# Ring places freed by a table of last steps for the first 48 chunks of the edge sums

## The reference

```
msg = feat[src] * a[:, :, None]                       # a row of 256 per edge
out = jax.ops.segment_sum(msg, dst, num_segments=N)   # first and last layer of this kind
agg = jax.ops.segment_sum(wbar[:, None] * msg, dst, num_segments=n)   # second: msg from feat[src] + edge features
```

## Time and profile before

| | |
|---|---|
| runs | 6173.45, 6169.5, 6158.29 us; median 6169.5 |
| profiled execution | 6167.76 us, of which the span of the profile is 6166.0 |
| busy in the span | PE 71%, DVE 45%, ACT 15%, POOL 28% |
| gathers in the first sum stage | start 598.9 to 947.8 us |
| gathers in the second sum stage | start 1864.0 to 2219.6 us |
| gathers in the third sum stage | start 5457.7 to 5796.5 us |

### The profile page before, as it was taken

The page is one execution under the profiler, slowest core; times in us unless marked ns, Lnnn a source line. Parts: engine busy times, 40 slices in busy tenths (PEclk is TensorE's granted clock), DMA queues, the critical chain, the costliest instruction groups (busy, mean ns, idle before and its releaser), DMA issues. The chain is left out here.

```text
span 6166.0 us, 74287 instructions
## 1 busy us (share of the span) xinstructions
PE 4377.0 (71%) x17651; PEld 3012.9 (49%) x17653; DVE 2769.8 (45%) x6598; ACT 908.0 (15%) x1973; POOL 1738.7 (28%) x1518
## 2 busy tenths in 40 slices
PE   0695985457916676766898999989936727766539
PEld 0463553235603444633566766667625715434337
DVE  4766445225685555687102011020141256664558
ACT  0200001111000012227102021020212310000012
POOL 2472771126707730100000000000021056547400
PEclk9897996557958787888999999999958968888759
DMA  3383873225818720013542433324222126624300
GB/s 115 104 242 120 266 243 107 72 75 155 244 41 260 240 86 16 3 59 161 178 129 68 139 100 110 122 66 134 64 83 65 57 61 184 195 79 128 94 27 21
DMA packets 438326, 726.18 MB, mean 118 GB/s; under 512 B 58253, under 2 KB 298698, under 8 KB 433698
## 3 DMA queue, kind: packets, MB, share of 16 engines
q1 hardware_dynamic: 318919, 513.08, 26.8%
q0 software_dynamic: 81376, 175.99, 9.5%
q10 hardware_dynamic: 37874, 35.28, 1.7%
HBM read 602.76 MB, written 121.12 MB: 117 GB/s over the span
## 5 line engine op out<-in xcount | busy, mean ns | idle before, releaser
L738 PE MATMUL gin_up_sums<-gin_ring,gin_acc 125*128 125x250 f32 (+1 forms) x4000 | 1069.5, 427 | 23.8 <-ACTq L771 23.8
L738 PEld LDWEIGHTS gin_up_sums<-gin_ring,gin_acc 125*128 125x128 f32 x4000 | 755.7, 189 | 332.0 <-ACTq L771 24.8
L720 DVE BATCH_NORM_STATS2 gin_up_stat<-gin_mlp_z x160 | 77.8, 486 | 1160.4 <-ACT gin_mlp_z L768 1160.2
L2255 POOL IOTA two_seats_pid<- 125x1 f32 x1 | 0.1, 138 | 1617.3 <-ACTq L2252 1617.3
L2824 PE MATMUL edge_sum_part<-edge_ring_rows,edge_sum_hot 128*125 x832 | 275.8, 486 | 142.9 <-DVE edge_sum_hot L1655 118.1
L2824 PE MATMUL loops_sum_part<-loops_ring_rows,loops_sum_hot 128*125 x832 | 272.5, 481 | 122.0 <-issue 81.8
L2940 POOL DMA_INDIRECT edge_ring_rows<-edge_table,src_e x243 | 282.9, 1164 | 239.6 <-PE edge_sum_part L2824 168.6
L2940 POOL DMA_INDIRECT gat_ring_rows<-gat_table,src_e x243 | 276.8, 1139 | 173.4 <-PE gat_sum_part L2824 105.5
L2940 POOL DMA_INDIRECT loops_ring_rows<-loops_table,src_e x243 | 266.3, 1096 | 176.2 <-PE loops_sum_part L2824 109.5
L2824 PEld LDWEIGHTS edge_sum_part<-edge_ring_rows,edge_sum_hot 128*125 128x125 f32 x832 | 164.4, 227 | 254.1 <-issue 234.8
L3170 PE MATMUL adj_counts_part<-adj_counts_far,adj_counts_low 128*128 128x325 bf16 x1032 | 210.4, 338 | 101.6 <-DVE adj_counts_far L3151 51.0
(11 more groups left out here) (800 smaller groups left out, 8008.6 us busy)
## 6 DMA issues: line engine op xcount, KB each, us to landing
gin_ring<-gin_adj SPq DMA_DIRECT2D x100, 937.5 KB, 4.8
gin_ring<-gin_adj SPq DMA_DIRECT2D x100, 625.0 KB, 3.9
edge_sum_own<-edge_attr_in SPq DMA_DIRECT2D x97, 512.0 KB, 4.8
gat_sum_ef<-edge_attr_t_in SPq DMA_DIRECT2D x96, 512.0 KB, 4.4
gin_adj<-adj_counts_tile SPq DMA_DIRECT2D x25, 1562.5 KB, 5.2
gat_logits_places<-lookup SPq DMA_DIRECT2D x32, 800.0 KB
edge_logits_places<-lookup SPq DMA_DIRECT2D x32, 800.0 KB
loops_logits_places<-lookup SPq DMA_DIRECT2D x32, 800.0 KB
```

Of the source, the lines that this page charges most:

```text
L720: v.bn_stats(statf[:, bass.ds(i * 12 + (h * 6 + f * UNITS * 6), 6)], z1f[:, nodes(i, h, f * N)]).then_inc(stats, 1)
L738: mm = pe.matmul(sums[h][k][:, 0:n * P].rearrange("p (t n) -> p t n", n=P), acc[:, t, k * 128:(k + 1) * 128], ring[0:P, q, 0:n, c * P:(c + ...
```

## The change

`prepare` keeps a table `g.free_at` of 48 entries: for old chunk c the first step of chunk c + 1, which is the count of steps after which chunk c is done, plus HOTS. A new function `place_free` reads the entry into a register for old chunks below KNOWN = 48 and waits on `summed` for it; then it increments a semaphore of its own and waits for that. From old chunk 48 on the wait is as before. POOL and SP both call it. The work per chunk, the ring and the order of the gathers stay the same.

```diff
+KNOWN = 48
...
                 v.wait_ge(past_ready, 1)
+                q.mark(v.tensor_scalar(g.free_at[:], begin[0:1, 1:KNOWN + 1], float(HOTS), None, ALU.add))
...
+        place_known, load_known = st.sem("place_known"), st.sem("load_known")
...
-                ahead.gather_rest(pool, ring, summed)
+                ahead.gather_rest(pool, ring, summed, place_known)
...
-                    ahead.load(sp, ring, c, summed, loaded)
+                    ahead.load(sp, ring, c, summed, loaded, load_known)
...
-    def load(self, eng, ring, c, summed, loaded):
+    def load(self, eng, ring, c, summed, loaded, known):
 
         if c in self.FIRST:
-            eng.wait_ge(summed, c + QUAD - 1 - RING + T + HOTS)
+            self.place_free(eng, c + QUAD - 1, summed, known)
...
-    def gather_rest(self, pool, ring, summed):
+    def place_free(self, eng, c, summed, known):
+
+        old = c - RING
+        if old < KNOWN:
+            eng.wait_ge(summed, eng.value_load(self.g.free_at[0:1, old:old + 1], min_val=1 + HOTS, max_val=old + 1 + T + HOTS))
+            eng.sem_inc(known, 1)
+            eng.wait_ge(known, old // QUAD // EVERY + 1 if c - QUAD + 1 in self.FIRST else old // QUAD - old // QUAD // EVERY)
+        else:
+            eng.wait_ge(summed, old + T + HOTS)
+
+    def gather_rest(self, pool, ring, summed, known):
 
         for q in range(RING, CS, QUAD):
             if q not in self.FIRST:
-                pool.wait_ge(summed, min(q + QUAD - 1, CS - 1) - RING + T + HOTS)
+                self.place_free(pool, min(q + QUAD - 1, CS - 1), summed, known)
...
+        g.free_at = sb("free_at", [1, KNOWN], I32)
```

More of the change, by code:

```diff
@@ L1647, in _ @@
                     sp.dma_start(own[:, c % OWN:c % OWN + n, :], feats_v[:, c:c + n, :]).then_inc(own_in[c % OWN // QUAD], 16)
-                    ahead.load(sp, ring, c + 2 * QUAD, summed, loaded)
+                    ahead.load(sp, ring, c + 2 * QUAD, summed, loaded, load_known)
             @block.vector
```

## The result

| | before | after |
|---|---|---|
| median of the runs | 6169.5 us (5 runs, 6158.29 to 6178.77) | 6132.87 us (5 runs, 6126.55 to 6135.61) |
| span of the profile | 6166.0 us | 6131.1 us |

The kernel became 36.6 us faster, a ratio of 0.9942 [0.9932, 0.9953]. Forecast (6137) and result agree to 4 us, but two terms behind it, the reads of the table and the pace of the gathers, were wrong in opposite directions. The stages show them.

The account below looks back on a forecast made before the run. POOL's gathers were taken to bound the three sum stages. 42.6 us won at the 37th gathers less 10.4 given back made 32.2, so 6137 us; own range 6120 to 6149, with rivals 6117 to 6162.

Parts of the forecast that it names:

- What bounds the stages: Three edge-sum stages: POOL never rests from first gather to last, so a stage ends with its last gather plus unchanged tail.
- When the places come free: First gather of each sum stage needs 8 steps instead of 32, so starts 21.0, 17.8 and 17.9 us earlier.
- The gate at chunk 116: The 37th gather still needs 80 steps; from there at most 14.7, 17.8 and 17.0 us can be won.
- The reads: Nine POOL table reads a stage at 0.43 us each, 3.9 us; range from 0 (hidden) to 12.3 us a stage.
- The gain at the 37th gather: How much earlier the 37th gather comes in the three stages: 14.7, 13.9 and 14.0 us, together 42.6.
- What is given back: Behind the 37th gather POOL's slow phase lasts longer, with dearer gathers: 5.3, 1.9 and 3.2 us lost, together 10.4.
- rival 1: First stage: two gathers lock to each TensorE quad, leaving 4.8 us won; with reads at 1.36 us, 6155 us; chance 0.22.
- my own mark for wrong: Signs against the forecast, among them gather distances over 1.65 us in the slow phase of a sum stage.
- The sum: Whole kernel: 42.6-10.4 = 32.2 us won, 6135.6 against the profiled execution, 6137 as median of the runs.
- Nothing comes of it: Rival 2: another server (the tail, DMA at 0.98) holds the stage ends, 6169 us; chance 0.05.
- slower: Rival 3: register waits stall POOL's queue before known quads; slower by 0.3% from 2.40 us each, 6204 at 3; chance 0.04.
- rival 4: Sum stages: reads hidden and little given back, 49.5 us won, 6120 us; chance 0.04.

Follow-up runs that it names:

- with constants: The changed kernel with the same earlier waits written as constants, without table read, increment or second wait: 6130.06 us, ratio 0.9935 to before.
- the experiment with one input: VectorE's multiplication by the weights made a one-input multiplication by 1, in the changed kernel and in the kernel before: 6096.48 and 6121.08 us.
- the cut kernels on the third chip: VectorE's multiplication and addition cut by two or four in the changed kernel, by four in before, by four with 80 known: 6344.09, 6348.87, 6341.7, 6344.9 us.

## Why the prediction was right

- **What bounds the stages: right.** POOL is the server from its first gather to its last. A third fewer gathers shortened the stages by 16%, and from before to after the last gather and the last matmul of a stage moved together to within 0.2 us.
- **When the places come free: right in the steps, short in the release.** The first gathers came at 8.9, 6.3 and 6.5 us into the stages; the forecast has 8.3, 6.0 and 5.8. The release was taken over at 0.28 us; over the register it is 0.85 in every stage, and with constants it is 0.27 again. The 0.57 us were left out of the sum by taking the increment and the second wait at nothing; no run separates them from the wait on a register. Relative to the stages 20.3, 17.5 and 17.2 us are won at the first gather.
- **The gate at chunk 116: right.** POOL waited at it in the first stage alone, and tables of 24 and 80 entries moved it as expected.
- **The reads: the size was off.** Nine reads were to cost 3.9 us a stage and cost none, the bound from below. The row at hand gave the duration rightly (435 ns), but not the place: the reads run beside the gathers. Eight times as many still gave the time of after. With reads at nothing the prediction's own sum is 6169.5-(14.7+17.8+17.0-10.4) = 6130.4, not the 6132 that it names for that case.
- **The gain at the 37th gather: 14.7, 13.9 and 14.0 forecast, 14.6, 15.7 and 15.3 measured.** The reads would have made it more, but the slow phase was slower than taken: 1.572 and 1.539 us a gather instead of 1.522 and 1.488, so 1.8 us over 36 gathers in the second and third stage. 17.5-1.8 = 15.7 and 17.2-1.8 = 15.4 are what was measured, to 0.1. I had carried the pace of before over unchanged.
- **What is given back: 5.3, 1.9 and 3.2 forecast, 8.4, -1.1 and 3.3 measured.** The mechanism is right in the first and third stage: the slow phase lasts longer. VectorE first waits for gathered rows 55 and 38 us behind the 37th gather; the forecast has 54 and 36. In the first stage the price of a slow gather was too small: the 24 gathers behind the 37th came 1.68 us apart instead of 1.574. Ahead of it the lock of rival 1 held for 26 gathers, and my own mark for wrong, over 1.65 us in the slow phase, was passed there with 1.733, or 1.68 without the gate's wait. That pace cost nothing at the 37th gather, because POOL still reached the gate with 2.13 us to wait; the loss is 3 us more than forecast behind it. In the second stage the last 206 gathers ran at 1.455 us instead of 1.460, which is the -1.1. But this stage took 387 to 394 us in the profiles of the kernels with 48 or more known and SyncE's old or new waits, so its 16.8 has a few us of scatter, and the pair of the experiment with one input gives 1.9 there.
- **The sum.** 42.6-10.4 = 32.2 us were forecast. Measured are 45.7-10.6 = 35.1 us: three more at the 37th, by hidden reads less a slower pace, and the same given back. The total of the second term agrees by cancellation, not by its parts, and that is luck.
- **The rivals.** Nothing comes of it, and slower, are out. The register waits would have had to cost 1.71 us each. They cost 0.57 at the three first gathers and showed no gap at the other 24. Of rival 1 the lock came, in one stage, but not its price. Of rival 4 the reads were hidden, but not little was given back.

## What to carry to other kernels

When a wait is too strict, follow its release to the next place where the old rule still holds. The gain is what is left at that gate, not what shows at the first instruction. Work on the sequencer's side in front of a queue of long instructions costs nothing as long as the queue is fed; price it at the moment when the queue is empty, which here was once a stage. And look at who serves: the same change was worth 36 us where POOL set the pace and nothing in the cut kernels on the third chip, where TensorE did.

## What the hardware showed beyond that

- A gather's 0.95 us on POOL becomes 1.94 when it starts just inside a VectorE multiplication of 1.22 us with two SBUF inputs, and 1.38 just inside one of 0.69 us with one SBUF input. Both end 0.81 to 0.82 us behind the end of the operation. Inside a copy of 0.69 us out of PSUM it kept its 0.94.
- Because of that, POOL can lock to TensorE's pace through VectorE: 1.94+0.95 us and two gaps of 0.30 make one quad of 3.49 us.
- A release that goes over a register-valued wait and the queue's own semaphore takes 0.85 us instead of 0.28.
- POOL's register reads ran ahead of its gathers, by up to 12 gathers that had not started.
- On one chip register operations of 36 ns on TensorE's queue took up to 1.40 us at a time. The three stages of a kernel with its multiplication cut in four took 171.7 us longer there than those of the uncut kernel on another chip, with the rest of the kernel within 5 us; how much of it is the chip is not shown apart from the 142 us by which the uncut kernel was slower there.
